# Two spectra with the sequences side by side, inverse transforms paired, and VectorE's gate moved ahead of the residual

## What is computed

```python
h = layernorm(x)
proj = (h @ in_proj_w + in_proj_b).reshape(B, L, C, 3)
v, gate = proj[..., 0], proj[..., 2]              # branch 1 is overwritten and drops out
v = short_conv(v, short_w) + short_b               # three taps along the sequence
filt = mlp(positions)[..., 1]                      # one filter of length L for each channel
conv = irfft(rfft(v, 2 * L) * rfft(filt, 2 * L))[:L]
x = x + (gate * conv) @ out_w + out_b
x = x + layernorm(x) @ (sum_k weights[k] * W[ids[k]]).T + mixed_bias
```

## Time and profile before

| | before |
|---|---|
| median of 3 runs | 2492.92 us (2491.86 to 2500.28) |
| the profiled execution's own time | 2495.54 us |
| span of the profile, first to last instruction | 2493.6 us |
| busy: TensorE, VectorE, ScalarE, GpSimd | 2372.5, 1554.6, 846.4, 912.1 us |
| mean granted TensorE clock | 0.977 of full speed |
| DMA, mean over the span | 199 GB/s |

### The profile page before, as it was taken

One profiled execution on the slowest core, in us unless ns is written; L12 is line 12 of the kernel. 1 busy time (PEld: TensorE's weight loads), 2 busy tenths in 40 slices (PEclk: granted clock), 3 DMA queues, 4 the chain that ended last, 5 costly groups with the idle time before them and its releaser, 6 DMA issues. The chain is left out here.

```text
span 2493.6 us, 39561 instructions
## 1 busy us (share of the span) xinstructions
PE 2372.5 (95%) x12804; PEld 1584.5 (64%) x12804; DVE 1554.6 (62%) x2188; ACT 846.4 (34%) x1151; POOL 912.1 (37%) x1189
## 2 busy tenths in 40 slices
PE   6779999999999999789999978999999999999998
PEld 2257777777777777533333335777777777777776
DVE  5734444343434444256777657788888888888875
ACT  3334343444444444234444442222222222222222
POOL 2322222222222222100000006666666666666664
PEclk9789999999999999899999999999999999999999
DMA  5534545445345545499999987755555555555553
GB/s 188 202 97 146 193 139 173 163 170 181 135 160 169 184 135 209 190 327 341 340 340 347 339 297 246 221 175 171 169 173 173 173 175 169 169 175 171 173 175 93
DMA packets 207925, 496.59 MB, mean 199 GB/s; under 512 B 18411, under 2 KB 18732, under 8 KB 190836
## 3 DMA queue, kind: packets, MB, share of 16 engines
q1 hardware_dynamic: 153588, 395.09, 49.2%
q10 hardware_dynamic: 54272, 100.68, 10.9%
HBM read 276.27 MB, written 219.43 MB: 199 GB/s over the span
## 5 line engine op out<-in xcount | busy, mean ns | idle before, releaser
L1052 DVE TENSOR_TENSOR m_m<-m_psA,m_spec 128x1024 f32<-128x1024 f32 x256 | 295.6, 1217 | 147.7 <-PE m_psA L957 133.6
L1212 ACT ACTIVATE b_z<-b_y,b_shift,b_rstd 128x512 f32<-128x512 f32 x128 | 104.4, 816 | 714.2 <-POOL b_shift L1179 714.2
L707 POOL TENSOR_TENSOR vl<-v,vh 128x512 fp32r<-128x512 f32 x128 | 165.7, 1295 | 403.7 <-ACT vh L661 403.7
L974 PE MATMUL m_psW<-m_m,mats 64*64 64x512 f32 x2048 | 252.1, 595 | 3.3 <-issue 3.3
L957 PE MATMUL m_psA<-m_xin,mats 64*64 64x512 f32 x1536 | 204.9, 605 | 35.3 <-DMA m_xin<-spec 27.1
L180 PE MATMUL b_psF<-wfh,b_zh 128*128 128x512 f32 x512 | 216.2, 422 | 3.4 <-DVE b_zl L1315 3.4
L180 PE MATMUL psV<-wvh,nth 128*128 128x512 f32 x512 | 216.3, 422 | 0.6 <-DVE ntl L789 0.6
L808 DVE TENSOR_TENSOR gto<-psG,bgr 128x512 f32<-128x512 f32 x128 | 87.7, 685 | 202.7 <-PE psG L182 202.5
L180 PE MATMUL b_psO<-woh,b_oh 128*128 128x512 f32 x512 | 211.8, 414 | 0.0
L181 PE MATMUL psV<-wvl,nth 128*128 128x512 f32 x512 | 203.5, 398 | 0.0
L182 PE MATMUL psV<-wvh,ntl 128*128 128x512 f32 x512 | 203.3, 397 | 0.0
(11 more groups left out here) (122 smaller groups left out, 4539.9 us busy)
## 6 DMA issues: line engine op xcount, KB each, us to landing
m_xin<-spec SPq DMA_DIRECT2D x31, 2304.0 KB, 14.6
spec<-fs1o SPq DMA_DIRECT2D x32, 2048.0 KB, 10.4
spec<-m_wo ACTq DMA_DIRECT2D x64, 1024.0 KB, 10.2
b_fin<-spec SPq DMA_DIRECT2D x128, 512.0 KB, 3.9
xg<-in_L_attn_x_dram SPq DMA_DIRECT2D x64, 512.0 KB, 6.2
gate_d<-gto SPq DMA_DIRECT2D x32, 1024.0 KB, 3.9
b_gin<-gate_d SPq DMA_DIRECT2D x128, 256.0 KB, 4.1
b_xin<-in_L_attn_x_dram SPq DMA_DIRECT2D x256, 128.0 KB, 3.5
```

What stands on the lines that cost most here:

```text
L707: pool.tensor_tensor(vl[:, t % 2], v[:, t % 2], vh[:, t % 2].bitcast(F32), ALU.subtract).then_inc(v_lo, 1)
L974: mm = pe.matmul(psW[pair % 2][half[slot], q, :], ws[slot][half[q]], m[half[q], pair % RM, part, slot, :], start=part == 0, stop=part == 1)
L1052: dve.tensor_tensor(m[:, (k - 2) % RM, part], psA[k % RA][:], spec[:, par, part], ALU.mult).then_inc(m_done, 1)
L1212: act.activation(z[:, t % 2], y[:, t % 2], ACT.Identity, bias=shift[:, t % 2:t % 2 + 1], scale=rstd[:, t % 2:t % 2 + 1]).then_inc(z_done, 1)
```

## The change

Three things change.

1. **Layout of the two spectra.** `spec1` was `[sequence, row, channel]` with the filter as a ninth sequence, and `spec3` `[sequence, row, channel]`. Now both are `[row, sequence, channel]`, and the filter has a tensor `spec_f` of its own. In the middle, a partition's eight sequences are then 16 KB in one piece for the load (they were pieces of 2 KB, 8 MB apart) and 8 KB in one piece for each store. The filter's piece is loaded by a DMA of its own. In the front, four tiles that a partition stores were 8 KB in one piece. Now they are four pieces of 2 KB, 16 KB apart, and the store is two DMAs, one for each half. Partitions are 512 KB apart there, where they were 64 KB apart, and so they are in `load_conv` of the back.
2. **`conv` in pairs.** TensorE does no `conv` in even rounds, and the `conv` of two tiles in a row at the start of an odd round.
3. **Orders in the back.** VectorE does `gate` ahead of `residual` in a round, and GpSimd `correct` ahead of `scalars`.

```diff
@@ -164,8 +164,9 @@
                          out_w, out_b, w_ad, b_ad, ids, weights, consts, out):
     ctx = ExitStack()
 
-    spec1 = nc.dram_tensor("spec1", [GB, ROWS * N2, C], F32, kind="Internal").ap()
-    spec3 = nc.dram_tensor("spec3", [B, ROWS * N2, C], F32, kind="Internal").ap()
+    spec1 = nc.dram_tensor("spec1", [ROWS * N2, B, C], F32, kind="Internal").ap()
+    spec_f = nc.dram_tensor("spec_f", [ROWS * N2, C], F32, kind="Internal").ap()
+    spec3 = nc.dram_tensor("spec3", [ROWS * N2, B, C], F32, kind="Internal").ap()
     gate_d = nc.dram_tensor("gate_d", [B, Q, P, SUB * C], F32, kind="Internal").ap()
     first_v = nc.dram_tensor("first_v", [B, C], F32, kind="Internal").ap()
     edge_f = nc.dram_tensor("edge_f", [2, P, T * C], F32, kind="Internal").ap()
@@ -299,7 +300,7 @@
                     sp.wait_ge(e1_done, t + 1)
                     sp.dma_start(edge_rows(1, t), e1[:, t % 3]).then_inc(e1_stored[t % 3], 16)
                     sp.wait_ge(s1_out, t + 1)
-                    sp.dma_start(spec1[B].rearrange("(r h t) c -> t r h c", h=2, t=T)[t], s1o[:, t % 2]).then_inc(s1_stored[t % 2], 16)
+                    sp.dma_start(spec_f.rearrange("(r h t) c -> t r h c", h=2, t=T)[t], s1o[:, t % 2]).then_inc(s1_stored[t % 2], 16)
                     if t in (3, 6):
 
                         kt = 2 + (3, 6).index(t)
@@ -610,8 +611,9 @@
                         return
                     slot = (t // SUB) % 2
                     sp.wait_ge(s_out, tile_no(b, t) + 1)
-                    sp.dma_start(spec1[b].rearrange("(r h t) c -> r h t c", h=2, t=T)[:, :, t - SUB + 1:t + 1, :],
-                                 s1o[:, slot]).then_inc(s_stored[slot], 16)
+                    rows = spec1.rearrange("(r h t) b c -> b h r t c", h=2, t=T)[b]
+                    for h in range(2):
+                        sp.dma_start(rows[h, :, t - SUB + 1:t + 1, :], s1o[:, slot, h]).then_inc(s_stored[slot], 16)
 
                 def store_gate(b, t):
                     if t % SUB != SUB - 1:
@@ -631,7 +633,7 @@
                 pipelined(sp, B, T, [(load_x, 0), (save_v0, 5), (load_adapter, 6), (store_gate, 8), (store, 9), (store_mix, 11)])
                 sp.wait_ge(ad_stored, 32)
                 for slot in range(2):
-                    sp.wait_ge(s_stored[slot], 16 * B * Q // 2)
+                    sp.wait_ge(s_stored[slot], 32 * B * Q // 2)
                     sp.wait_ge(g_stored[slot], 16 * B * Q // 2)
                 sp.wait_ge(v0_out, 16 * B)
 
@@ -665,7 +667,7 @@
                     act.wait_ge(s_ps, tile_no(b, t) + 1)
                     if t % SUB == 0 and old(b, t, 2 * SUB):
 
-                        act.wait_ge(s_stored[slot], 16 * (b * (Q // 2) + t // (2 * SUB)))
+                        act.wait_ge(s_stored[slot], 32 * (b * (Q // 2) + t // (2 * SUB)))
                     act.activation(s1o[:, slot, :, t % SUB], psS[t % 2][:], ACT.Copy).then_inc(s_out, 1)
 
                 def s_pair(b, t):
@@ -884,10 +886,9 @@
 
             def rows_of(spec_dram, g):
 
-                by_group = spec_dram.rearrange("b (g p) c -> g p b c", p=P)
                 if isinstance(g, int):
-                    return by_group[g]
-                return by_group[bass.ds(g, 1)].rearrange("g p b c -> (g p) b c")
+                    return spec_dram[g * P:(g + 1) * P]
+                return spec_dram[bass.ds(g * P, P)]
 
             @block.sync
             def _(sp):
@@ -900,12 +901,14 @@
                     if at_first(i, s):
 
                         for k, piece in enumerate(PIECES):
-                            sp.dma_start(xin[:, par, piece], rows_of(spec1, 0)[:, piece]).then_inc(first_in[k], 16)
+                            src = rows_of(spec1, 0)[:, piece] if k else rows_of(spec_f, 0).rearrange("p (b c) -> p b c", b=1)
+                            sp.dma_start(xin[:, par, piece], src).then_inc(first_in[k], 16)
                         return
                     if not at_first(i, s, 2):
 
                         sp.wait_ge(a_ps, (group(i, s) - 1) * PAIRS)
-                    sp.dma_start(xin[:, par], rows_of(spec1, group(i, s))).then_inc(x_in[par], 16)
+                    sp.dma_start(xin[:, par, B], rows_of(spec_f, group(i, s))).then_inc(x_in[par], 16)
+                    sp.dma_start(xin[:, par, 0:B], rows_of(spec1, group(i, s))).then_inc(x_in[par], 16)
 
                 def load_consts(i, s):
 
@@ -937,7 +940,7 @@
                         if first:
                             pe.wait_ge(first_in[0], 16)
                         else:
-                            pe.wait_ge(x_in[par], 16 * (i + par))
+                            pe.wait_ge(x_in[par], 32 * (i + par))
                             pe.wait_ge(m_done, 2 * (g * PAIRS - 1))
                     elif k == 1:
                         if not first:
@@ -1143,7 +1146,7 @@
                 def load_conv(b, t):
                     if old(b, t, 2):
                         sp.wait_ge(c_ps, no(b, t) - 1)
-                    sp.dma_start(fin[:, t % 2], spec3[b].rearrange("(r h t) c -> t r h c", h=2, t=T)[t]).then_inc(f_in[t % 2], 16)
+                    sp.dma_start(fin[:, t % 2], spec3.rearrange("(r h t) b c -> b t r h c", h=2, t=T)[b, t]).then_inc(f_in[t % 2], 16)
 
                 def load_gate(b, t):
                     if old(b, t, 2):
@@ -1195,7 +1198,7 @@
                         pool.wait_ge(res_done, no(b, t) - D + 1)
                     pool.tensor_tensor(yb[:, t % D], y[:, t % 2], bfr[:], ALU.add).then_inc(yb_done, 1)
 
-                pipelined(pool, B, T, [(scalars, 3), (bias_y, 3), (correct, 0)])
+                pipelined(pool, B, T, [(correct, 0), (scalars, 3), (bias_y, 3)])
 
             @block.scalar
             def _(act):
@@ -1236,6 +1239,12 @@
                     for h in range(2):
                         mm = pe.matmul(psC[t % 2][h * N1:(h + 1) * N1, :], s4[:, h * T + t, :], fin[:, t % 2, h, :], start=True, stop=True)
                     mm.then_inc(c_ps, 1)
+
+                def conv_pair(b, t):
+
+                    if t % 2:
+                        conv(b, t - 1)
+                        conv(b, t)
 
                 def turn_o(b, t):
                     pe.wait_ge(o_done, no(b, t) + 1)
@@ -1271,7 +1280,7 @@
                                  wfh[:, ct], wfl[:, ct], ct == 0, ct == CT - 1)
                     mm.then_inc(ff_ps, 1)
 
-                pipelined(pe, B, T, [(conv, 1), (adapt, 5), (turn_o, 1), (turn_z, 4), (project, 2)])
+                pipelined(pe, B, T, [(conv_pair, 0), (adapt, 5), (turn_o, 1), (turn_z, 4), (project, 2)])
 
             @block.vector
             def _(dve):
@@ -1321,7 +1330,7 @@
                         dve.wait_ge(out_stored[t % D], 32 * (b * (T // D) + t // D))
                     dve.tensor_tensor(res[:, t % D], psF[t % 2][:], yb[:, t % D], ALU.add).then_inc(res_done, 1)
 
-                pipelined(dve, B, T, [(residual, 3), (gate, 1), (finish, 5), (o_low, 1), (z_low, 4), (bias_x, 0)])
+                pipelined(dve, B, T, [(gate, 1), (residual, 3), (finish, 5), (o_low, 1), (z_low, 4), (bias_x, 0)])
 
 
     with ExitStack() as st:
```

## The result

The changed kernel takes **2578.82 us** (median of 4 runs, 2569.21 to 2591.45) against 2492.68 us for the kernel before, a ratio of 1.0342 with an interval of 1.0305 to 1.0379. It is slower, as forecast, but by 86 us and not by 164. The profiled execution took 2591.45 us, 95.9 us more than the profiled one of before, and its trace is what I read. It is the slowest of the four, 12.6 us above the median, so that what I read in it adds up to 96 us and not to 86. What makes the four differ by 22 us no trace shows.

What follows compares the result with a forecast made beforehand. It took TensorE and a ring of dependences across VectorE, GpSimd and ScalarE, level at about 7.6 us a round, to bound the back. 2495.5 + 174 - 12 + 2 = 2659.5, 2657 us on the median's scale; own range 2609 to 2726 us.

Steps and rivals of the forecast that it cites:

- the ring: Back: closed loop from `residual` through `bias_x` to the next tile's `residual`, without TensorE, about 7.6 us, level with TensorE.
- New round: 7.56 + 1.44 = 9.00 us: Back: old round of 7.56 us plus `gate`'s two operations, 1.44 us, against 7.62 us now.
- +174: Back: `gate` ahead of `residual` adds 1.38 us in each of 126 rounds; ends +141 and +227 us.
- a bound (0.2 us): Back: 0.2 us less a round if `scalars` gets faster by what it lost beside `gate`, giving 8.74 us and +141 us.
- Nothing: Back, GpSimd: `correct` ahead of `scalars` only turns the list and costs nothing; without that cover `gate` would wait for it.
- The pairs hide: Back, TensorE: paired convs save 0.10 to 0.15 us a round, hidden by 1.4 us to spare: nothing.
- The middle: Middle: bigger load pieces remove half of at most 25 us, -12 us, since no row tells the two ends apart.
- The whole 25 us: Middle: most that bigger pieces can remove, 30 x 0.84 us; by the skill's rule all of it would be won.
- The front and its seam: Front: smaller store pieces hide; the last store before the middle does not, +2 us, bounds 0 and +6.
- store of the front as the bound: Front, rival: stores take 28 us instead of 10.4, some 2780 us; chance 0.03.
- a lower clock: Back, rival: idling TensorE is granted 1.2 GHz, giving 2750 us or more; chance 0.04.
- TensorE waits for `b_o` in every round: Back, expected sign in the profile after: TensorE waits for `b_o` ahead of `b_psP` in every round.

Runs made afterwards that it cites:

- norm_last: The changed kernel with ScalarE's `norm` moved behind `o_high` and `z_high` in the back: 2455.24 us, 0.9842 of the kernel before.
- before_norm_last: The kernel before with only ScalarE's `norm` moved behind `o_high` and `z_high`: 2492.16 us, ratio 0.9987.
- one_correct: The changed kernel without the second of GpSimd's two operations of `correct` (the subtraction): 2483.46 us, 0.9955 of the kernel before.
- pool_back: The changed kernel with GpSimd's order of before (`scalars`, `bias_y`, `correct`): 2629.96 us, 1.0537 of the kernel before.
- gate_alone: The kernel before with VectorE's `gate` ahead of `residual` and nothing else: 2641.66 us, ratio 1.0593.
- layout_alone: The kernel before with the new layout of both spectra and nothing else: 2474.66 us, ratio 0.9921.
- spec1_alone: The kernel before with the new layout of `spec1` and `spec_f` only: 2474.02 us, ratio 0.9921.
- gate_back: The changed kernel with VectorE's order of before, `residual` ahead of `gate`: 2502.06 us, 1.0026 of the kernel before.
- pair_alone: The kernel before with the convs in pairs and nothing else: 2521.90 us, ratio 1.0106.
- biasx_shadow: The changed kernel with `bias_x` directly behind `residual` on VectorE: 2496.83 us, 1.0002 of the kernel before.

## Why the prediction was half right

**The direction and the mechanism were right.** `gate` went into the ring of residual, scalars, norm, o_high, o_low, z_low and bias_x. `b_corr` follows `b_xin` with no idle time, `b_y` follows `b_o`, the wait ahead of `b_ol` is 2.02 us (1.8 forecast), the clock stays at 1.00, and norm_last shows that this ring and no other costs the time. One reading was too strong: that in most rounds of the kernel before nothing but the ring set the time. With the ring open these rounds still last 7.63 us (before_norm_last), so TensorE alone sets them as long, and the ring was at most level with it.

**The step that failed is the size of the new round**, "New round: 7.56 + 1.44 = 9.00 us". It is 8.50 us, and the term +110 us where +174 stood. Three things make up the 0.50:

- `gate` costs 1.32 us from `b_corr` to `b_y`, not 1.44: the 0.03 us that I added behind each operation are not there behind `b_o`. It starts at 1862.55 and takes 0.69 us, and `b_y` starts at 1863.16, before `b_o` has ended. 0.12 us.
- The old ring without `gate` beside it isn't 7.56 but 8.70 - 1.32 = 7.38 us. `b_y` to `b_z` fell from 3.48 to 3.11, because the last operation of `scalars` no longer has `b_o` beside it (first row: before; second: changed kernel). I named this as a bound (0.2 us) and did not take it into the value. 0.18 us. Together these make 8.70, which the second of the three kinds of rounds shows.
- `bias_x` I took at its 1.72 us in every round, from one row. It is short in a third of them. (39 x 7.96 + 57 x 8.71 + 25 x 8.87) / 121 = 8.50, the last 0.20 us. Over 126 rounds these are 25 of the 30 us by which 2578.82 us lies under the forecast's own range from 2609; the lowest round in that range was 8.74 us. In the changed kernel the price of that operation has two values, with GpSimd's `correct` as the cause (one_correct). In the kernel before it lies anywhere from 0.68 to 1.82 us, and its profile already gives 1457 ns as the mean over 128, where the row that I took has 1.79 us.

```profile
1861.89 0.56 POOL L1179 TENSOR_TENSOR b_shift<-b_shift,b_rstd 128x1 f32<-128x1 f32 x1
...
1866.05 0.19 POOL L1182 TENSOR_TENSOR b_shift<-b_shift,b_rstd 128x1 f32<-128x1 f32 x1
```

**`correct` ahead of `scalars`: "Nothing" was wrong in its size.** It is worth 51 us within this change (pool_back), by the cover that the sentence behind it named: with it, `gate` does not wait for GpSimd.

**The pairs hide: not shown here, wrong in general.** With a ring of 8.5 us or more a pair's round of about 8.4 us should hide in it, but no run takes the pairs out of the changed kernel. The nearest runs speak for a small price: pool_back, which is gate_alone with the pairs and the layout, is 12 us faster than gate_alone, where the layout alone gives 21. My "if TensorE were the bound, 15 us would be won" is 19 us when the rings are open and minus 26 us when one of 7.1 us is closed. I had looked at the mean load of TensorE and not at its two rounds.

**The middle**: -12 us was forecast within 0 to -25, and it is -21 (layout_alone), 0.64 of the 0.84 us a group. spec1_alone puts all of it on the layout of `spec1`. The whole 25 us, which I worked out from a rule of the Trainium skill, page "DMA: Bandwidth & Descriptors", section "Latency and other measured facts", are nearer than my half. This is no test of that rule, which speaks of the pitch between partitions: in the load of before the partitions were 2 KB apart, and only the pieces of one partition 8 MB. Pieces and pitches changed together here, so that no run tells which of them it was. The profiled execution of the change shows 14 us ahead of the back, and that of layout_alone 21: there the middle's first load is issued at 1040.39 us and not at 1044.47, and its second load keeps TensorE waiting 10.4 us and not 12.0. Why they differ, no run shows.

**The front and its seam**: two stores of 1024 KB land after 8.7 us and hide, as forecast, and the middle's first load is issued 0.45 us later than before. `b_fin` lands after 4.4 us instead of 3.9 and hides as well. A store of the front as the bound did not come. Nor did a lower clock that costs anything: windows of 10 us from 1570 and from 2490 us have a granted clock of 0.83, but the rounds there last 7.94 to 8.71 us, no longer than elsewhere.

**TensorE waits for `b_o` in every round** was wrong in its place: it waits above all for `b_zl` ahead of `adapt` (152.9 us), and for `b_o` in 74 of some 119 rounds, 34.6 us. Both come out of the same ring, `b_zl` first in TensorE's order.

**What stays open**: what decides whether `bias_x` comes first. The pairs have to do with it: in the changed kernel 36 of the 39 short rounds, from `b_y` to `b_y`, are among the 61 in which TensorE starts a pair of convs, and of the 60 others only 3 are short. Without pairs `bias_x` is under 1 us in 2 of 128 rounds (gate_alone), and in gate_back and pair_alone nearly always. How the pair shifts the two starts, which lie 0.01 us apart in the rows shown, is not shown, and no run set that distance on purpose.

## What to carry to other kernels

When every engine works through a hand-written list, draw the ring of dependences *with* the list's order in it, before pricing anything. A step moved into a ring costs its whole length in every round, and the cure can be one entry in another engine's list: here `norm` behind `o_high` turned a loss of 3.4% into a gain of 1.6%. Where an engine's load is uneven from round to round, its shortest round must be held against every ring, and not its mean: here 6.55 us against a ring of 7.15. And a duration from one row should be looked up over all rounds: an operation with two durations is meeting something.

## What the runs showed of the hardware

The same `bias_x` takes 0.68 or 1.81 us and GpSimd's operation 1.84 or 1.28, by which of them comes first. The starts in the two cases read 1852.15 against 1852.14 and 1860.10 against 1860.09, so that the profile's start times don't tell who won, only the lengths do. Taking the GpSimd operation away gained 95 us of 2579. GpSimd's small operations of one element a partition are hit too: 0.19 us alone and 0.55 beside `bias_x` (biasx_shadow), 0.19 alone and 0.56 beside `b_o` (the kernel before).
